# Attention on one core: where a rotary projection stands among the products of a group, and in which order VectorE takes its work

## The reference

```
h = layernorm(x) * (1 + ca) + sa
x = x + ga * attention(h)
h = layernorm(x) * (1 + cb) + sb
x = x + gb * ffn(h)
```

## Time and profile before

| | us |
|---|---|
| median of 3 runs | 906.31 (899.53 to 908.09) |
| the profiled execution | 895.69 |
| its span, first to last instruction | 894.0 |
| around the span | 1.69 |
| PE busy | 813.2 (91%) |
| DVE busy | 637.1 (71%) |
| ACT busy | 397.2 (44%) |
| POOL busy | 662.7 (74%) |

### The profile page before, as it was taken

How to read it: one execution, slowest core, us unless ns; L and a number is a source line. 1 busy time by engine, 2 the same in 40 slices (tenths; PEclk the granted TensorE clock), 3 DMA queues, 4 the chain that set the end, 5 groups by cost and what they waited for, 6 DMA issues and landing times.

```text
span 894.0 us, 14690 instructions
## 1 busy us (share of the span) xinstructions
PE 813.2 (91%) x5118; PEld 485.9 (54%) x5118; DVE 637.1 (71%) x1156; ACT 397.2 (44%) x650; POOL 662.7 (74%) x348
## 2 busy tenths in 40 slices
PE   4689999999999999999999999999999977968581
PEld 2445555555555555555555555555555444368581
DVE  8987777777777777777777777777776757646022
ACT  3654444444444444444444444444444433336340
POOL 2579998898987878787878787878777856632333
PEclk8979999999999999999999999999999999969796
DMA  9101001010101011111011111101010000078683
GB/s 246 31 1 14 13 14 25 14 25 13 25 13 26 13 26 14 27 20 26 6 26 25 22 25 14 24 14 14 13 13 15 12 13 1 19 238 269 213 314 89
DMA packets 84330, 43.91 MB, mean 49 GB/s; under 512 B 57632, under 2 KB 73376, under 8 KB 84192
## 3 DMA queue, kind: packets, MB, share of 16 engines
q1 hardware_dynamic: 83232, 40.86, 18.2%
q0 software_dynamic: 1024, 2.10, 0.7%
HBM read 36.51 MB, written 6.16 MB: 48 GB/s over the span
## 4 chain that ended last, share of the span: by engine, by line
PE 82%; DVE 8%; DMA 4%; POOL 2%; issue 2%; ACT 1%; POOLq 0%; SPq 0%; DVEq 0%
PE ps_o L456 25%; PE ps_m L422 9%; PE ps_x L410 8%; PE ps_s L440 7%; PE ps_s L442 6%; PE ps_s L446 6%; PE ps_s L444 6%; PE ps_s L473 3%; DMA moe<-xs_dram 3%; PE ps_s L464 3%; PE ps_s L595 2%; PE ps_s L586 2%; POOL xs_dram L953 2%; DVE mx L1097 1%; PE ps_s L377 1%
## 5 line engine op out<-in xcount | busy, mean ns | idle before, releaser
L939 POOL TENSOR_TENSOR acc<-acc,probs 128x1024 f32<-128x1024 f32 (+1 forms) x192 | 459.9, 2395 | 74.7 <-ACT probs L697 52.5
L1097 DVE TENSOR_REDUCE mx<-ps_m 128x2 f32<-128x1024 f32 x240 | 293.7, 1224 | 90.9 <-PE ps_m L422 90.3
L697 ACT ACTIVATE probs<-ps_s 128x1024 f32<-128x1024 f32 x256 | 248.8, 1024 | 157.7 <-PE ps_s L446 157.6
L456 PE MATMUL ps_o<-probs,c_all 128*64 128x512 f32 x1024 | 249.5, 608 | 0.0
L440 PE MATMUL ps_s<-q_hi,k_hi 64*128 64x512 f32 x512 | 102.6, 397 | 12.0 <-DVE x_sb L1153 12.0
L456 PEld LDWEIGHTS ps_o<-probs,c_all 128*64 128x64 f32 x1024 | 62.4, 136 | 93.2 <-issue 44.5
L422 PE MATMUL ps_m<-k_hi,q_hi 64*128 64x512 f32 x480 | 107.7, 444 | 4.0 <-DVE mx L1097 4.0
L939 POOL TENSOR_TENSOR acc<-probs 128x1024 f32<-128x1024 f32 (+1 forms) x32 | 75.4, 2357 | 48.3 <-ACT probs L697 47.8
L442 PE MATMUL ps_s<-q_hi,k_lo 64*128 64x512 f32 x512 | 101.4, 391 | 0.0
L446 PE MATMUL ps_s<-neg_row,one_row 64*128 64x512 f32 x512 | 101.3, 391 | 0.0
L444 PE MATMUL ps_s<-q_lo,k_hi 64*128 64x512 f32 x512 | 100.8, 389 | 0.0
(11 more groups left out here) (299 smaller groups left out, 1025.5 us busy)
## 6 DMA issues: line engine op xcount, KB each, us to landing
probs<-in_experts SPq DMA_DIRECT2D x15, 578.0 KB, 6.0
rr<-rd_dram SPq DMA_DIRECT2D x62, 128.0 KB, 3.1
wu<-in_wqk SPq DMA_DIRECT2D x16, 256.0 KB, 3.4
neg_row<-nm SPq DMA_DIRECT2D x256, 0.5 KB, 2.0
w_first<-in_experts SPq DMA_DIRECT2D x5, 578.0 KB, 5.2
rot<-in_experts SPq DMA_DIRECT2D x5, 578.0 KB, 5.0
hT<-in_experts SPq DMA_DIRECT2D x5, 578.0 KB, 5.6
xs_dram<-zero SPq DMA_DIRECT2D x2, 960.0 KB, 9.4
```

The costliest lines, as they stand in the source:

```text
L456: ins = nc.tensor.matmul(ps_o[64 * h:64 * h + 64, :], c_all[:, (p // HP) * TB + kt, :], probs[:, st % 4, h, :], start=(kt == 0), stop=(kt ...
L697: nc.scalar.activation(probs[:, st % 4, :, :], ps_s[:, 2 * (st % 2):2 * (st % 2) + 2, :], ACT.Exp, scale=SCALE).then_inc(s["probs"], 1)
L939: V.tensor_tensor(acc[:, half, heads, :], first, probs[:, st % 4, heads, :], ALU.add).then_inc(s["added"], 1)
L1097: V.reduce_max(mx[:, :, kh, qt], max_banks(q, n), AX.X).then_inc(s["max_reduced"], 1)
```

## The change

In the attention loop of three engines instructions change places; none is added, removed or resized.

- PE: `up(p + 2, g)` moves ahead of maxima product b.
- ACT: `upper` moves behind the two exponentials, and takes the unit of the same group (`upper(p + 2, g)`) where it took that of the group before.
- DVE: `turn(p + 2, g)` moves between the two `reduce_max`, and `lower` behind the second (and behind `neg_max` in groups 3 and 7), for the unit of the same group.

The order in one group, after:

- PE: maxima a, score, score, up(g), maxima b, pv, pv.
- DVE: reduce a, turn(g), reduce b, lower(g).
- ACT: expo, expo, upper(g).

```diff
@@ PE
                     score(p, 2 * g)
                     score(p, 2 * g + 1)
+                    if p + 2 <= LAST:
+                        up(p + 2, g)
                     if p < LAST:
                         maxima(p + 1, 2 * g + 1)
...
-                    if p + 2 <= LAST:
-                        up(p + 2, g)
                     for n in (2 * g - 2, 2 * g - 1):
                         if n >= 0:
                             pv(p, n)
@@ ACT
-                    if g == 0 and 2 <= p + 1 <= LAST:
-                        upper(p + 1, NGRP - 1)
-                    if g > 0 and p + 2 <= LAST:
-                        upper(p + 2, g - 1)
                     expo(p, 2 * g)
                     expo(p, 2 * g + 1)
+                    if p + 2 <= LAST:
+                        upper(p + 2, g)
@@ DVE
                     if p < LAST:
                         reduce_max(p + 1, 2 * g)
-                    q, u = (p + 2, g - 1) if g else (p + 1, NGRP - 1)
-                    if 2 <= q <= LAST:
-                        lower(q, u)
+                    if p + 2 <= LAST:
+                        turn(p + 2, g)
                     if p < LAST:
                         reduce_max(p + 1, 2 * g + 1)
                         if g % 4 == 3:
                             neg_max(p + 1, g // 4)
                     if p + 2 <= LAST:
-                        turn(p + 2, g)
+                        lower(p + 2, g)
```

## The result

The changed kernel takes 975.62 us (median of 4 runs, 972.96 to 976.39) against 903.71 us (4 runs) for the kernel before: a ratio of 1.079, 95% interval 1.0727 to 1.0853. That is slower, as forecast, but by 72 us instead of 41, and outside the range (929 to 962). The profiled execution took 975.25 us, its span is 973.5 us.

A forecast was written before the change was run, and what follows sets the result against it. The prediction took PE as the bound before, and a PE-DVE loop through turn after. 84 groups at 0.47 us (39.5) plus 1.5 for the first gave 41 us on the 906.3 median: 947 us, range 929 to 962.

The forecast's parts named there:

- The closed loop: Short groups: maxima a, scores, up, turn, reduce b, next maxima a wait in a ring; 5.50 us against 5.03.
- the term for them: Short groups: each takes 5.50 less 5.03 us, 0.47 more; 39.5 us over 84 groups.
- The sign that the prediction named: Waits list: PE's maxima wait for DVE's reduce, 0.3 to 0.6 us in some 85 groups, about 40 us in all.
- Rival 1: Up on PE had really waited for lower, so the change gains 10 to 39 us: 867 to 896; chance 0.03.
- The long groups: Groups 3 and 7: denominators and outputs add 1.96 us, so PE stays the bound and their time holds within 0.2 us.
- Shapes on PE: Up ahead of maxima b moves a change of tile shape: 0 less to 0.1 us more a group, 0.2 allowed.
- Pair 0: First group, without value products, goes from 3.98 to 5.50 us, 1.5 more; its short groups lose 0.47 each.
- rival 3: PE's new stands drop the clock to 1.2 GHz: 1150 us if in all 84 groups, 967 in one of ten; chance 0.03.
- The rule of the Trainium skill: Attention loop: short idle times between matmul groups can make the clock swing; weighed against the change, with the time of rival 3.
- Rival 2: DVE: denominators come 1.5 us later, so reciprocals in groups 0 and 4 block reduce a; worst case 975 us; chance 0.07.
- The slack of 1.2 us: DVE: reduce a would end at 1.77 us and turn cannot start before 3.0, so late reciprocals cost nothing.
- seven terms: One short group, maxima a round to the next: 0.30, 1.61, 0.32, 0.78, 0.78, 0.35 and 1.36 us, sum 5.50.

The follow-up runs named there:

- second try: Changed kernel with up first in the group, lower ahead of reduce b, division on GpSimd, reciprocals ahead of reduce b of groups 1 and 5: 902.15 us, ratio 0.9984.

## Why the prediction was right and wrong

*The closed loop: right.* Forecast 5.50 us, measured 5.53, term by term. Turn back behind reduce b opens it (5.24), and PE's old order with turn ahead gives 5.74 to 5.79, where the same sum makes 5.73. Of the 71.5 us the short groups of pairs 1 to 13 have 38.5; the term for them was 78 x 0.47 = 37. The sign that the prediction named, maxima waiting for some 40 us in all, came as 44.7, but by luck: the stands in the short groups are 0.23 us, under the 0.3 to 0.6 that it gave, and the long groups, where it had none, bring 20.

*Rival 1, up had really waited for lower: fell.* Lower (L1088) now ends at 443.27 and up comes at 445.36, 2.1 us later; yet up's weight load stands 0.35 us in each of 112 groups, put down to issue now (39.6 us in the waits list). So it is not the wait on lower. That it is the change of tile shape is still argued, from where the 0.35 us stand; no run shows it.

*The long groups: wrong, and this is the step that failed.* The prediction put it so: "there PE stays the bound, and these groups keep their time (0 to 0.2 us either way for the shapes)". They took 1.04 us more, 27 us in all. The shapes are 0.21 of it (5.5 us), at the edge of the bound. The other 0.83 (21.6 us) is the division: the two runs that keep it from GpSimd's addition bring the long groups to 7.19, and the time down by 20 us, to 955 and 956, which is within the forecast range. The prediction does not name the division at all. With "No instruction is added, so all the price is in order and waits" it took every duration as given. This one was not; it hung on the moment at which the division starts.

*Shapes on PE: mis-sized.* The prediction had "About nothing for PE, 0 less to 0.1 more a group". With both waits out of the way up's place costs 0.21 us in every group. In the changed kernel's timeline up starts 2.26 after maxima a, maxima b 0.66 later, the value products 0.44 later still: 3.36, where the earlier trace rows has 3.16. The term from maxima b to the value products, which the prediction set at 0.32, is 0.44, and up to maxima b is 0.66, at the upper end of its 0.55 to 0.67. In short groups of the changed kernel it is hidden, since there the loop ends last.

*Pair 0: half right.* The prediction had 4.3 us here (1.5, and 0.47 in six groups); 5.9 came. The first group took 5.53 for 5.50. The second took 6.87 instead of 5.5: in a stand of 2.1 us just ahead of it (the longest in the row of PE's waits above) the clock fell. From 70 to 74 us the changed kernel's granted clock was

```profile
70.00:74.00 4.00, 2.72 (x13) 2.35 (x15) 2.69 (x4) 0.56 (x2) 1.57 (x1) 0.60 0.24 66
74.00:750.00 676.00, 636.49 (x3846) 364.33 (x3844) 505.81 (x769) 287.85 (x386) 508.58 (x229) 1.00 0.09 16
```

a mean of the two levels, 1.2 and 2.4 GHz. So what rival 3 names came at one place, for some 1.4 us. That the change brought this on is not shown: with the division on GpSimd in the kernel before, whose pair 0 is the same as before, the granted clock was 0.58 from 61 to 65 us, and the first group took 5.40 us for 3.98. With the stands of 0.23 and 0.77 us in the other groups the clock stays at 1.00. The rule of the Trainium skill that the prediction weighed, that short idle times between groups of matmuls can make the clock swing (TensorE: Matmul & The Clock Gate, "A second HAM failure mode: psum-queue depth-cycling"), is not borne out by this loop: the granted clock is 1.00 from 74 to 750 us.

*Rival 2, the reciprocals: fell for this kernel.* They wait in 28 places, 19.1 us in all, where it was 10 and 6.9, and groups 1 and 5 take 5.53 us like the rest. The slack of 1.2 us was enough. With up first the same waits did cost time, as the second try shows. In the run of the DVE and ACT parts alone groups 1 and 5 are longer too, which only its trace puts down to them.

*What holds the division up.* Single instructions, first the kernel before (a division and GpSimd's two additions around it), then an addition of the changed kernel:

```profile
405.57 2.38 POOL L939 TENSOR_TENSOR acc<-acc,probs 128x1024 f32<-128x1024 f32 x1
...
407.83 0.68 DVE L1144 TENSOR_TENSOR ou<-ou,rr 128x512 f32<-128x512 f32 x1
...
408.09 2.68 POOL L939 TENSOR_TENSOR acc<-acc,probs 128x1024 f32<-128x1024 f32 x1
```

```profile
448.18 2.38 POOL L937 TENSOR_TENSOR acc<-acc,probs 128x1024 f32<-128x1024 f32 x1
```

The addition of the changed kernel ends at 450.56, and the division (448.73 + 2.39 = 451.12) 0.56 later; in all 26 places up to pair 13 it ends 0.55 to 0.56 us behind an addition's end. The program has the division wait for its reciprocals and for the copied sums, not for the addition that runs beside it. Its duration follows the time that the addition has left at its start, with 0.55 us on top, in all orders: 0.94 us for 0.39 (one place of the kernel before), 1.41 for 0.86 (turn back), 2.28 for 1.73 (up's place alone), 2.39 for 1.84 (the changed kernel). So it does nothing while the addition runs. In the kernel before an addition ended at 407.95, 0.12 after the division's start, and the next one, which began in the middle of the division, took 2.68 us instead of 2.38: there it was GpSimd that waited, for 0.3 us.

The Trainium skill (SBUF — State Buffer, "Who interferes with whom") says that a VectorE instruction with two inputs in SBUF reads the second through a port that it shares with GpSimd, that this access is locked for a whole instruction, and that whoever comes later is blocked. The runs here agree: both inputs of the division lie in SBUF, and it waited up to 1.85 us; turn, whose first input lies in PSUM, took its 0.42 to 0.43 us beside running additions in both kernels. That the port is the cause is the page's word; the runs show that the two instructions exclude each other.

## What to carry to other kernels

Where an engine's queue is reordered, look for loops that close through two engines and add them up from one trace; here seven terms from rows gave 5.50 us where 5.53 came. Then look at the durations that the reordering assumes fixed. One instruction here took 0.68 us or up to 2.7, by what GpSimd did beside it, and a mean well above the median (0.81 and 0.68 us for the division before) was the sign of it. Here a shift in phase, from 0.1 to 1.8 us ahead of an addition's end, was worth some 20 us.

## What I had not expected

In the kernel before the division started 0.07 to 0.16 us ahead of an addition's end in 25 of its first 26 places, though nothing in the program orders the two. Its row had the price in it all the same: a mean of 813 ns over 31, since two in pair 14 took 2.4 and 2.7 us. Nor had I expected what a caught division can do further on: in the run of up's place alone, 1.6 us more on DVE became 2.0 us a long group on PE, and 3.7 us in the 18 where the clock went down to 1.2 GHz behind the stand of 2 us.
